# Convolution stage of a graph network on one core: the one-hot marks of the sources on GpSimd, the broadcast rows in bytes

## What is computed

```
h = gelu(concat(x[src], x[dst]) @ mlp_w1 + mlp_b1)
edge_weight = sigmoid(h @ mlp_w2 + mlp_b2)
deg  = segment_sum(edge_weight, dst) + 1
dinv = rsqrt(deg)
msg  = (x @ conv_w)[src] * dinv[src] * edge_weight * dinv[dst]
out  = segment_sum(msg, dst) + dinv**2 * (x @ conv_w) + conv_b
```

## Time and profile before

| | |
|---|---|
| median of three runs | 6839.37 us (6838.39 to 6848.54) |
| the profiled execution | 6857.47 us, of which the span from first to last instruction 6855.8 us |
| TensorE, matmuls | 3609.7 us busy, 53% |
| VectorE | 3138.8 us, 46% |
| ScalarE | 1361.7 us, 20% |
| GpSimd | 3608.0 us, 53% |
| bytes moved by DMA | 1036.18 MB, 151 GB/s over the span |
| `edges_conv` in the trace | from about 4453 to about 5005 us |

### The profile page before, as it was taken

One profiled execution on the slowest core, in us unless ns is written; L12 is line 12 of the kernel. 1 busy time (PEld: TensorE's weight loads), 2 busy tenths in 40 slices (PEclk: granted clock), 3 DMA queues, 4 the chain that ended last, 5 costly groups with the idle time before them and its releaser, 6 DMA issues. The chain is left out here.

```text
span 6855.8 us, 83075 instructions
## 1 busy us (share of the span) xinstructions
PE 3609.7 (53%) x18454; PEld 2698.3 (39%) x18454; DVE 3138.8 (46%) x6417; ACT 1361.7 (20%) x3486; POOL 3608.0 (53%) x3745
## 2 busy tenths in 40 slices
PE   2444223345555555564665666366644666666662
PEld 2222222233333333333554555245522555555551
DVE  3444222216566666522333333299842444444445
ACT  0011111121111111130110111066641211111121
POOL 4777666556555656536666666400045555555542
PEclk6555555667777777775555555598865666666665
DMA  5555555325555555414555555299944555555541
GB/s 153 159 161 155 156 153 164 105 77 164 156 160 155 159 159 160 131 48 128 143 143 139 143 145 144 64 298 301 293 140 129 157 156 156 151 154 156 153 136 39
DMA packets 841337, 1036.18 MB, mean 151 GB/s; under 512 B 235200, under 2 KB 553104, under 8 KB 841235
## 3 DMA queue, kind: packets, MB, share of 16 engines
q1 hardware_dynamic: 489300, 485.89, 23.7%
q0 software_dynamic: 145888, 323.13, 18.4%
q10 hardware_dynamic: 206046, 226.10, 9.5%
HBM read 672.31 MB, written 362.35 MB: 151 GB/s over the span
## 5 line engine op out<-in xcount | busy, mean ns | idle before, releaser
L519 POOL DMA_INDIRECT L_gath<-tab_kv,src x832 | 789.5, 949 | 653.0 <-DVE L_pv L1268 404.7
L519 POOL DMA_INDIRECT L_gath<-tab,src x832 | 818.3, 984 | 542.4 <-DVE L_sent L816 290.4
L519 POOL DMA_INDIRECT L_gath<-in_x,src x832 | 822.2, 988 | 389.9 <-issue 242.3
L519 POOL DMA_INDIRECT L2a_gath<-tab_h,src x832 | 788.5, 948 | 451.6 <-issue 413.0
L612 DVE TENSOR_TENSOR_SCAN L_acc<-L_mask,L_acc,L_pT 128x512 f32<-128x512 bf16 x414 | 527.4, 1274 | 760.0 <-DMA set_tails<-in_dst 611.4
L629 ACT ACTIVATE L_back<-L_pB 128x512 f32<-128x512 f32 x624 | 365.4, 586 | 1411.4 <-DMA set_xs<-in_x 886.2
L911 PE MATMUL L2a_pZ<-w_M,L2a_hid 64*128 64x1 f32 x1664 | 385.7, 350 | 491.1 <-DVE ew_sb L932 331.5
L600 PE MATMUL L_pB<-ident,L_acc 128*128 128x128 f32 x2496 | 506.1, 340 | 252.7 <-issue 125.9
L911 PEld LDWEIGHTS L2a_pZ<-w_M,L2a_hid 64*128 64x128 f32 x1664 | 369.8, 325 | 573.7 <-issue 503.9
L922 DVE TENSOR_TENSOR_SCAN L2a_dest<-L2a_same,L2a_dest,L2a_pS 64x512 f32<-64x512 bf16 x207 | 262.9, 1270 | 706.2 <-remote 506.1
L600 PEld LDWEIGHTS L_pB<-ident,L_acc 128*128 128x128 f32 x2496 | 393.7, 180 | 442.3 <-issue 412.4
(11 more groups left out here) (280 smaller groups left out, 6467.4 us busy)
## 6 DMA issues: line engine op xcount, KB each, us to landing
run<-L_back ACTq DMA_DIRECT2D x416, 256.0 KB
L_seed<-seed SPq DMA_DIRECT2D x416, 256.0 KB
run<-L_back ACTq DMA_DIRECT2D x208, 264.0 KB
L_mask<-same SPq DMA_DIRECT2D x416, 128.0 KB
seed<-L_zeros SPq DMA_DIRECT2D x208, 256.0 KB
sent<-L2a_gath ACTq DMA_DIRECT2D x208, 256.0 KB
L_sent<-sent SPq DMA_DIRECT2D x208, 256.0 KB
run<-L_back SPq DMA_DIRECT2D x208, 256.0 KB
```

What stands on the lines that cost most here:

```text
L519: gp.indirect_dma_start(out=gath[k][:, t, :], out_offset=None, in_=table, in_offset=bass.IndirectOffsetOnAxis(ap=g["src"][:, tile:tile + 1 ...
```

## The change

VectorE no longer builds the two marks. GpSimd does, in an order of its own with no loop (`steps`): hot(n) and then hot_of_high(n), the latter as four instructions of 128x49 with one number a partition to compare with, where VectorE had one of 128x196. For these numbers `high` becomes float32. GpSimd begins once VectorE has prepared `lane`, `row` and `high`. VectorE's list keeps pick(n-1), gather_up(n-1), scan(n-3), times_weight(n-1).

The tables `low` and `same8` (a new copy of `same`) have one byte a number, and so have the tiles `low` and `mask` of this phase. The other phases go on reading `same`. `setup` makes the copy on VectorE and stores it with one more transfer. In `edges_conv`, SP increments a semaphore `mgo` after the wait for the slot and before each of the two loads; nothing waits for it.

```diff
-        g["low"] = dram("low", [EP], BF16)
+        g["low"] = dram("low", [EP], U8)
+        g["same8"] = dram("same8", [EP], U8)
...
+            sp.dma_start(chunk(g["same8"]), same8[:, :]).then_inc(s_w, 16)
...
+            v.tensor_copy(same8[:, :], g["same_c"][:, :])
...
-        mask, low = slot("mask", [P, BE], BF16), slot("low", [P, BE], BF16)
+        mask, low = slot("mask", [P, BE], U8), slot("low", [P, BE], U8)
...
-        high = ph.sb("high", [P, TILES], BF16)
+        high = ph.sb("high", [P, TILES])
...
-            pipeline(sp, BATCHES, SLOTS, [(0, mask_load(sp, g["low"], low, s_low, s_hotl)), (0, load),
-                                          (2, mask_load(sp, g["same"], mask, s_mask, s_scan)), (8, store_rows(sp, run, back, s_back, s_out))])
+            pipeline(sp, BATCHES, SLOTS, [(0, mask_load(sp, g["low"], low, s_low, s_hotl, s_mgo)), (0, load),
+                                          (2, mask_load(sp, g["same8"], mask, s_mask, s_scan, s_mgo)), (8, store_rows(sp, run, back, s_back, s_out))])
...
+            gp.wait_ge(s_prep, 4)
+
+            def hot(n, k, r):
+                landed(gp, s_low, k, r)
+                room(gp, s_look, n, SLOTS)
+                gp.tensor_scalar(hot_low[k][:, :], low[k][:, :], lane[:, 0:1], None, ALU.is_equal).then_inc(s_hotl, 1)
+
+            def hot_of_high(n, k, r):
+                room(gp, s_part, n, SLOTS)
+                for t in range(BT):
+                    a = gp.tensor_scalar(hot_high[k][:, t, :], row[:, :], high[:, n * BT + t:n * BT + t + 1], None, ALU.is_equal)
+                a.then_inc(s_hoth, 1)
+            steps(BATCHES, SLOTS, [(0, hot), (0, hot_of_high)])
...
-            v.wait_ge(s_prep, 4)
-
-            def hot(n, k, r):
-                landed(v, s_low, k, r)
-                room(v, s_look, n, SLOTS)
-                v.tensor_scalar(hot_low[k][:, :], low[k][:, :], lane[:, 0:1], None, ALU.is_equal).then_inc(s_hotl, 1)
-
-            def hot_of_high(n, k, r):
-                room(v, s_part, n, SLOTS)
-                v.tensor_tensor(hot_high[k][:, :, :], row[:, :].unsqueeze(1).to_broadcast([P, BT, HIGH]),
-                                high[:, bass.ds(n * BT, BT)].unsqueeze(2).to_broadcast([P, BT, HIGH]), ALU.is_equal).then_inc(s_hoth, 1)
-
...
-            pipeline(v, BATCHES, SLOTS, [(0, hot), (1, pick), (0, hot_of_high), (1, gather_up), (3, running_sum(v, pT, mask, acc, s_turn, s_mask, s_ret, s_scan)),
+            pipeline(v, BATCHES, SLOTS, [(1, pick), (1, gather_up), (3, running_sum(v, pT, mask, acc, s_turn, s_mask, s_ret, s_scan)),
...
-def mask_load(sp, table, mask, s_mask, s_free):
+def mask_load(sp, table, mask, s_mask, s_free, s_go=None):
 
     def load(n, k, r):
         room(sp, s_free, n, SLOTS)
+        if s_go:
+            sp.sem_inc(s_go, 1)
```

More of the change, by code:

```diff
@@ L8 @@
 BF16 = mybir.dt.bfloat16
+U8 = mybir.dt.uint8
 ALU = mybir.AluOpType
@@ L246, in setup @@
         part = [ph.sb(f"part{j}", [1, bias_all], BF16) for j in range(3)]
-        src, low = ph.sb("src", [P, TILES], I32), ph.sb("low", [P, TILES], BF16)
+        src, low, same8 = ph.sb("src", [P, TILES], I32), ph.sb("low", [P, TILES], U8), ph.sb("same8", [P, TILES], U8)
         heads, tails, opens = ph.sb("heads", [1, TILES], I32), ph.sb("tails", [1, TILES + 1], I32), ph.sb("opens", [1, 2, TILES], BF16)
@@ L288, in _ @@
                 sp.dma_start(g["bias"][j:j + 1, :], part[j][:, :]).then_inc(s_w, 16)
-            sp.wait_ge(s_w, 16 * (len(loads) + 12))
+            sp.wait_ge(s_w, 16 * (len(loads) + 13))
         @block.scalar
@@ L654, in edges_conv @@
         pL = [ph.ps(f"pL{k}") for k in range(2)]
-        s_iota, s_prep, s_hotl, s_hoth, s_look, s_part, s_pick, s_scale, s_turn, s_scan, s_ret, s_back, s_sum = (ph.sem(n) for n in
-            ("iota", "prep", "hotl", "hoth", "look", "part", "pick", "scale", "turn", "scan", "ret", "back", "sum"))
+        s_iota, s_prep, s_hotl, s_hoth, s_look, s_part, s_pick, s_scale, s_turn, s_scan, s_ret, s_back, s_sum, s_mgo = (ph.sem(n) for n in
+            ("iota", "prep", "hotl", "hoth", "look", "part", "pick", "scale", "turn", "scan", "ret", "back", "sum", "mgo"))
         s_mask, s_low, s_sent, s_out = (ph.slot_sems(n, SLOTS) for n in ("mask", "low", "sent", "out"))
```

## The result

The changed kernel takes 6937.76 us (median of four runs, 6932.7 to 6947.6) against 6839.48 before: 1.0144 times as long, with an interval of 1.0130 to 1.0158. That is 98 us more, where 26 less were forecast, and above the upper end of the range, 6872. It is rival (c): GpSimd became the bound. Its five instructions take 3.07 us of each batch, and none of the bounds named in the prediction held, the one "from above" (2.27 us) included.

What follows compares the result with a forecast made beforehand. SP's queue was taken as next bound: 2.47 us plus 0.02 for the chain, 2.49 a batch against 2.62. That saves 0.13 x 208 = 27 us, less 1 for setup: 6839.4 to 6813 us, eight-in-ten range 6782 to 6872.

Steps and rivals of the forecast that it cites:

- rival (c): Convolution stage: GpSimd becomes the bound, from 2.62 us for its five instructions; at 2.9 us, 6898 us; chance 0.14.
- the one "from above": Upper bound on GpSimd's five comparisons a batch, a select's 284 ns all counted per column: 2.27 us.
- GpSimd's price: GpSimd's five comparisons a batch, priced from the slope of its selects: 1.47 us, between 1.1 and 2.27.
- the estimate made with it: GpSimd's five comparisons by the skill's 1.8 cycles per element, 768 ns for 512, with 0.22 for each small one: 1.65 us.
- the chain: Convolution: `low` transfer, comparison, look-up, scale, weigh, then SP's next issues; 2.46 us a batch before, 2.2 after the change.
- SP's 2.47: SP's queue issuing a batch's four transfers: floor 2.35 us plus 0.12 for two increments, range 2.39 to 2.55.
- three floors: Kernel before, per batch: VectorE 2.32 us, SP's queue 2.35, the chain 2.46, just below the measured 2.62.
- Rival (a): SP's queue costs less, increments at 0.02 us and waits hidden: 2.39 us a batch, -48 us, 6792; chance 0.12.
- The transfers: Halved `low` and `mask` save 0.18 to 0.53 us a batch: DMA occupancy from 2.46 to 1.93-2.28, taken as 2.1.
- Rival (b): Transfers cost per packet, not per byte, so relief is not passed on: 2.56 to 2.62 us, 6827 to 6840; chance 0.22.
- The scan on bytes: VectorE's scan reading a one-byte mask: no change taken, bounded by 0 and 0.27 us.
- Rival (d): VectorE's scan and GpSimd's comparison exclude each other: at least 2.88 us a batch, +54 us, 6893; chance 0.06.

Runs made afterwards that it cites:

- this version: Changed kernel with the higher mark back on VectorE, only the lower on GpSimd, rows in bytes: 6850.27 us against 6850.37 for the kernel before, ratio 1.0000.
- one lag: Kernel before with SP issuing the load of `sent` two batches later, nothing else: 5590.58 us against 5639.2, ratio 0.9912.
- The runs that show them bare: `sent` two batches later, in the kernel before (ratio 0.9912) and with the lower mark on GpSimd, rows in bytes (0.9956, both against the kernel before).
- the run that has nothing else: Kernel before with only the two semaphore increments on SP, ahead of the loads of `low` and `mask`: 5647.85 us against 5645.41, ratio 1.0003.
- the bytes run: Changed kernel with both marks back on VectorE, rows in bytes and the two increments kept: ratio 1.0004 to the kernel before.
- the runs with a cheap GpSimd: Changed kernel with only the lower mark, only the higher, or neither on GpSimd, the rest on VectorE: ratios 1.0000, 1.0002, 1.0004 to the kernel before.
- the fastest version: `low` and `mask` in one transfer, lower mark on GpSimd, higher on VectorE, `sent` two batches later: 5524.88 us against 5639.2 for the kernel before, ratio 0.9797.

## Why the prediction was wrong, point by point

**GpSimd's price: the step that failed.** The prediction took 1.47 us for the five instructions, bounded by 1.1 and 2.27; they take 3.07. The rows behind it were of another instruction, and the bound "from above" was one only if a comparison costs no more than a select. It counted 284 ns of 128 columns as 2.2 ns a column and nothing besides; measured are about 2.5 ns a column and nearly 0.3 us an instruction on top. The prediction said itself that no row shows a comparison on GpSimd, and then gave all such cases 0.14. With a price seen in no row, the point from which it decides (2.62 us for five, 1.8 times the value taken) was near, not far. The Trainium skill ("GPSIMD Engine Reference", 3.1) gives its 1.8 cycles an element as the best case of a tight loop; the estimate made with it, 1.65 us, was low as well, and the measured 1,564 ns for 512 columns are twice its 768.

**The bound that takes over: the second step that failed, hidden by the first.** Even at 1.57 us of GpSimd work the time does not move (1.0000). The prediction gave the chain 10.9 us for five batches, 2.2 us each, and took SP's 2.47 as what is late next. The chain takes 13.10. Against the terms of the sum: the transfer 4.22 where 4.24 stood; the comparison 1.58 and not 0.6; `part` to the end of `scale` 2.28 and not 1.87, of which about 0.27 is the higher mark, which this version has on VectorE between the two; SP's steps with the increments 1.96 and not 1.84; the look-up and the hand-overs 1.78 and not 1.1, of which 0.67 are between `weigh` and the issue of `sent`, where SP is often still at work on what stands ahead. The largest is GpSimd's price once more, 1.0 of 2.2 us; the rest is 1.2 us of small terms. The median transfer went from 4.38 us to 4.04 in this version and 3.98 with the bytes alone.

**The first reading of what bounds the kernel before** found three floors near one another and a measured time above all of them. The right one among them was the chain, and its 2.46 us were read from a single round of 12.31 us. Of the same interval taken over 170 batches that is the fourth shortest; the mean is 13.09 us (12.12 to 14.77). So the chain is not a floor below the measured time; it is the measured 2.62. Loosening it by one lag gives 2.40 a batch; the DMA share then goes to 0.98.

**SP's queue.** Floor 2.35, with the increments 2.47. The runs that show them bare have 2.40 and 2.52. The two increments cost SP 0.12 us a batch, as taken: from `sent` to the next `low` it needs 1.84 us without them and 1.96 with them, also in the run that has nothing else. Alone in the kernel before they cost no time that can be measured. Rival (a), with 2.39 us for SP, is refuted.

**The transfers.** The sum 0.94 x 2.62 = 2.46, less 0.18 to 0.53 us a batch: with bytes it is 0.80 x 2.68 to 0.83 x 2.62, 2.14 to 2.17, so 0.3 us were saved, inside the bounds. The packets of the traces show the same: from 4500 to 4950 us one of 1,024 bytes takes 58 ns in the mean before and one of 512 bytes 35 ns in the bytes run, about 22 ns less, where 11 to 33 were reckoned; one of 2,048 bytes goes from 93 to 97. Rival (b) said that this relief is not passed on, and in the runs with a cheap GpSimd it was not; but its reason was another. The transfers did become cheaper, and `low` landed 0.3 us sooner; with the rows in bytes on VectorE the longer comparison and the increments took that back.

**The scan on bytes** costs nothing (1,273 against 1,269 ns), as taken. What bytes do cost, 0.13 us on VectorE's own comparison, does not enter the changed kernel, which has it on GpSimd.

**Rival (d), exclusion.** The scan and a comparison do run side by side: 1,273 ns with GpSimd at 100%. What the rule of the Trainium skill names ("SBUF — State Buffer", Who interferes with whom: two SBUF inputs against a GpSimd read) is in the trace at the size of a detail. In the changed kernel `scale` takes 142 ns in the median and at most 548. In the run with the lower mark on GpSimd, VectorE's higher mark, which reads `row` and `high` from SBUF, shows min, median and max:

```profile
L719 DVE TENSOR_TENSOR L_hoth<-L_row,L_high x208: 343/352/804, 4460.6 to 5000.4; 128x196 bf16<-128x196 bf16 x104
```

Before, the same instruction went up to 356 ns. `scale`, the other with two inputs from SBUF, has 127/136/585 there, and every one of the 67 that are more than 40 ns longer than the median overlaps a comparison of GpSimd (so do 220 of the other 349). The trace agrees with the rule that such pairs meet, but a wait for the whole of a 1.56 us comparison never shows: the longest delay is 0.45 us.

## What to carry to other kernels

Price an instruction on an engine that has never run it in this kernel as unknown over a factor, not as its nearest neighbour: five instructions at twice the guess turned the forecast gain into a loss. When several floors lie a little below the measured time, look for the chain that goes round through a queue's order, count it over many rounds and not over one, and test it with a lag before taking work off engines; a load that waits for its slot holds everything issued behind it, here `low` of the next batch.

## What the runs showed of the hardware

GpSimd's comparison against one value a partition: 409, 941 and 1,564 ns for 49, 256 and 512 columns, at 512 the same for bytes and bf16. The large one takes up to 1.8 us in the run where VectorE's higher mark, with two SBUF inputs, runs beside it, and at most 1,585 ns in the changed kernel.

VectorE's comparison of 512 columns: 350 ns on bf16 and 483 on bytes; the scan does not tell them apart. In the run with the higher mark on GpSimd, a few comparisons of either engine are longer: VectorE's up to 746 ns (median 482), GpSimd's small ones up to 733 (median 410).

SP, issuing transfers in a loop: 2.40 us for four with their waits, and 0.06 us for each increment of a semaphore.

TensorE's granted clock fell in the changed kernel although it did less: 0.63 and 0.69 in the windows above, where the kernel before has 1.00 and 0.81 and the fastest version 0.99. The two levels are 1.2 and 2.4 GHz; of the stage, the changed kernel has 466 us at the lower and 181 at the higher, the kernel before 141 and 411. In the changed kernel TensorE stood still before the looks of nearly every batch, 139.9 of 450 us and up to 1.8 us at a time; in the fastest version it did more work in the same time and waited 81.6 of 300 us, 68.6 of them in waits of at most 0.8 us; its longest wait is 1.3 us. What decides was not tested. It is part of no sum here: at 3.07 us a batch GpSimd has no gap that a faster TensorE could close.
